# Smoothed int8 layers of a decoder: magnitudes and input integers on ScalarE, roots and weight steps spread from a repeated column

## What is computed

```python
def _smooth_quant_linear(x, w):
    amax_x = max(|x|, axis=0); amax_w = max(|w|, axis=0)
    s = maximum(sqrt(maximum(amax_x, EPS) / maximum(amax_w, EPS)), EPS)
    xs = x / s;  ws = w * s
    x_scale = maximum(max(|xs|, axis=-1), EPS) / 127      # one per row
    w_scale = maximum(max(|ws|, axis=-1), EPS) / 127
    x_q = clip(round(xs / x_scale)); w_q = clip(round(ws / w_scale))
    return x_q @ w_q.T * x_scale * w_scale.T

h = _smooth_quant_linear(x, guw); gate, up = split(h, 2, axis=-1)
a = silu(gate) * up
y = _smooth_quant_linear(a, dw)
```

## Time and profile before

| | |
|---|---|
| median of 3 runs | 1121.04 us (1120.28 to 1121.95) |
| the profiled execution | 1115.83 us, its span 1114.0 us |
| DVE busy | 862.6 us, 77% of the span |
| ACT busy | 555.0 us, 50% |
| PE busy | 798.0 us, 72% |
| the stage that the change touches | about 608.8 to 851.8 us of the span |

### The profile page before, as it was taken

One profiled execution on the slowest core, in us unless ns is written; L12 is line 12 of the kernel. 1 busy time (PEld: TensorE's weight loads), 2 busy tenths in 40 slices (PEclk: granted clock), 3 DMA queues, 4 the chain that ended last, 5 costly groups with the idle time before them and its releaser, 6 DMA issues.

```text
span 1114.0 us, 15206 instructions
## 1 busy us (share of the span) xinstructions
PE 798.0 (72%) x5063; PEld 322.0 (29%) x5063; DVE 862.6 (77%) x1155; ACT 555.0 (50%) x971; POOL 102.3 (9%) x220
## 2 busy tenths in 40 slices
PE   1456987999999999999356244533454266999997
PEld 1422321222222222223111022212224143444443
DVE  6999999999999999985999888898888574322111
ACT  4846324888888888885080024223233652754000
POOL 2110010000000000100000010000101052000001
PEclk9778995999999999999658556666567677999999
DMA  8400770111111121110300011010007402000000
GB/s 300 154 0 1 231 265 30 45 55 52 49 56 44 53 57 45 54 38 16 116 0 1 0 38 38 19 29 1 0 1 290 163 2 76 1 1 1 19 29 29
DMA packets 48323, 66.73 MB, mean 60 GB/s; under 512 B 11532, under 2 KB 25868, under 8 KB 47768
## 3 DMA queue, kind: packets, MB, share of 16 engines
q1 hardware_dynamic: 46488, 61.95, 16.9%
q0 software_dynamic: 1792, 4.22, 1.1%
HBM read 42.52 MB, written 19.19 MB: 55 GB/s over the span
## 4 chain that ended last, share of the span: by engine, by line
PE 46%; DVE 36%; issue 8%; ACT 6%; POOL 2%; DMA 1%; ACTq 1%; POOLq 0%; SPq 0%; DVEq 0%
PE PS L1302 11%; PE PS L1483 8%; PE PS L1493 7%; PE PS L1319 7%; PE PS L1271 5%; PE PS L1238 2%; ACT slab L1590 2%; DVE slab L999 2%; DVE slab L956 2%; DVE SWV L855 2%; DVE stats L663 2%; DVE HB L927 2%; ACT HB L1581 2%; DVE slab L989 2%; DVE mn L690 1%
## 5 line engine op out<-in xcount | busy, mean ns | idle before, releaser
L855 DVE TENSOR_REDUCE SWV<-PS 128x2 f32<-128x1024 f32 x256 | 303.3, 1219 | 22.2 <-PE PS L1271 18.8
L1590 ACT ACTIVATE slab<-PS 128x512 f32<-128x512 f32 x512 | 273.4, 600 | 77.7 <-PE PS L1319 71.6
L1302 PE MATMUL PS<-slab,HB 128*32 128x256 f32 x2048 | 157.6, 392 | 5.9 <-ACT HB L1581 5.9
L1319 PE MATMUL PS<-slab 50*128 50x512 f16 x512 | 139.4, 387 | 12.8 <-ACT slab L1590 10.5
L1271 PE MATMUL PS<-slab 48*128 48x512 f16 x512 | 103.9, 403 | 11.3 <-DVE SWV L855 10.2
L1483 PE MATMUL PS<-slab 128*128 128x512 f16 x384 | 86.5, 389 | 1.4 <-DVE slab L1138 1.4
L1493 PE MATMUL PS<-slab 128*128 128x512 f16 x384 | 83.0, 379 | 0.0
L1611 ACT ACTIVATE slab<-slab,rnd,inv 128x512 f32<-128x512 f32 (+1 forms) x32 | 20.0, 696 | 108.9 <-DVE inv L985 108.9
L1302 PEld LDWEIGHTS PS<-slab,HB 128*32 128x32 f32 x2048 | 45.0, 108 | 77.0 <-issue 70.0
L1153 DVE SCALAR_TENSOR_TENSOR slab<-HB,cmax,slab 128x512 f16<-128x512 f32 x32 | 24.1, 752 | 53.7 <-ACT slab L1658 53.7
L1319 PEld LDWEIGHTS PS<-slab 50*128 50x128 f16 x512 | 39.0, 94 | 72.7 <-ACT slab L1590 66.7
(11 more groups left out here) (273 smaller groups left out, 1227.4 us busy)
## 6 DMA issues: line engine op xcount, KB each, us to landing
slab<-in_L_ffn_w SPq DMA_DIRECT2D x2, 4096.0 KB, 13.6
q_split<-slab SPq DMA_DIRECT2D x24, 256.0 KB, 2.7
k_split<-slab SPq DMA_DIRECT2D x24, 256.0 KB, 2.8
slab<-q_split SPq DMA_DIRECT2D x64, 96.0 KB, 2.5
slab<-k_split SPq DMA_DIRECT2D x64, 96.0 KB, 2.5
slab<-in_x SPq DMA_DIRECT2D x4, 1024.0 KB, 12.3
slab<-HB SPq DMA_DIRECT2D x128, 32.0 KB
slab<-in_fside_BxS2xS SPq DMA_DIRECT2D x4, 1024.0 KB, 5.3
```

The costliest lines, as they stand in the source:

```text
L855: nc.vector.tensor_reduce(NM[:, ring].rearrange("p (a x) -> p a x", a=2)[:, :, x], PS[:, bank:bank + 2, :], AX.X, ALU.max, negate=True).th ...
L1302: ins = nc.tensor.matmul(PS[32 * h:32 * h + 32, 6, cols], VST[:, r % 2, k, h, :], PROB[:, k, h, cols], start=k == half == 0, stop=k == KB ...
L1319: nc.tensor.matmul(PS[:, st_bank(2 * s + a), :], KP[rows, r, p, P * k:P * k + P], QP[rows, r, p, :], start=True, stop=True).then_inc(st_re ...
L1590: nc.scalar.activation(PROB[:, k, 2 * a + p], PS[:, st_bank(t), :], ACT.Exp, scale=score_scale).then_inc(probs, 1)
```

## The change

Four things are changed in the stage.

- Column maxima (weights of every step, inputs of wide steps): ScalarE writes magnitudes into two buffers, `ABSW` and `ABSX`, in place of WB's contents (free by then); VectorE takes the larger of tiles 0, 1 and 2, 3 and then of the two results (two `tensor_tensor` instead of one reduction). Inputs of narrow steps keep the reduction.
- ScalarE's magnitudes of the weights of step n + 1 stand at the top of its work for step n, that is behind all of its work for step n - 1.
- No diagonals are built. TensorE takes a column repeated 128 times as weights and the identity as moving operand, one 128-column matmul for each block: eight for the roots of a wide step, four for a narrow one, and four for the row of weight steps. VectorE's L968 and GpSimd's L598 are gone.
- The input's integers are made by ScalarE, ahead of the weights' integers, in the same five-instruction form.
- The loads of router, b1 and b2 wait for the last weights' maxima, and GpSimd's constants for the routing wait likewise, since they write to WB.

```diff
             def weight_maxima(n):
-                dve.wait_ge(lw_in[n % 4], 16 * (n // 4 + 1))
-                nc.vector.tensor_reduce(LWM[chain(n)][:, 0:width(n)],
-                                        LW[chain(n)][layer(n)].rearrange("p t d -> p d t"), AX.X, ALU.max,
-                                        apply_absolute_value=True).then_inc(l_wmax, 1)
+                dve.wait_ge(l_wabs, n + 1)
+                largest_of_tiles(LWM[chain(n)][:, 0:width(n)], absolute(ABSW, n), l_wmax)
...
+            def largest_of_tiles(dst, a, signal):
+                own(nc.vector.tensor_tensor(a[:, 0:2], a[:, 0:2], a[:, 2:4], ALU.max))
+                nc.vector.tensor_tensor(dst, a[:, 0], a[:, 1], ALU.max).then_inc(signal, 1)
...
-                own(nc.vector.reciprocal(roots[:, 0, 0:ic], roots[:, 1, 0:ic]))
-                nc.vector.tensor_tensor(DIAG[c][:, 0:2, 0:w].rearrange("p a (i q) -> p a i q", q=P),
-                                        identf[:, :].unsqueeze(1).unsqueeze(1).broadcast_to([P, 2, ic, P]),
-                                        roots[:, :, 0:ic].unsqueeze(3).broadcast_to([P, 2, ic, P]),
-                                        ALU.mult).then_inc(l_diag, 1)
+                nc.vector.reciprocal(roots[:, 0, 0:ic], roots[:, 1, 0:ic]).then_inc(l_roots, 1)
...
-                for t in range(4):
-                    ins = nc.vector.tensor_scalar(xi[:, t], xi[:, t], lin[c][:, 0, t:t + 1], ROUND, ALU.mult, ALU.add)
-                own(ins)
-                nc.vector.tensor_scalar(LXQ[c][layer(n)], xi, ROUND, None, ALU.subtract).then_inc(l_xq, 1)
...
+            def in_every_row(bank, column):
+                return nc.tensor.matmul(bank, column.broadcast_to([P, P]), identf[:, :], start=True, stop=True)
+
             def spread_roots(n):
...
                 for a in range(2):
-                    nc.tensor.matmul(PS[:, 4 * c + 2 + a, 0:w], ones[:, :], DIAG[c][:, a, 0:w], start=True,
-                                     stop=True).then_inc(l_row, 1)
+                    for i in range(width(n) // P):
+                        ins = in_every_row(PS[:, 4 * c + 2 + a, P * i:P * i + P], roots[:, a, i:i + 1])
+                    ins.then_inc(l_row, 1)
...
+            def magnitude_of_w(n):
+                act.wait_ge(lw_in[n % 4], 16 * (n // 4 + 1))
+                if n:
+                    act.wait_ge(l_wmax, n)
+                nc.scalar.activation(absolute(ABSW, n), LW[chain(n)][layer(n)], ACT.Abs).then_inc(l_wabs, 1)
...
             for n in range(LSTEPS):
-                c, a = chain(n), layer(n)
+                if n + 1 < LSTEPS:
+                    magnitude_of_w(n + 1)
+                    if layer(n + 1) == 0:
+                        magnitude_of_x(n + 1)
+                c, a, xi = chain(n), layer(n), xin(n)
                 act.wait_ge(l_scale, n + 1)
+                for t in range(4):
+                    nc.scalar.activation(xi[:, t], xi[:, t], ACT.Identity, bias=rnd[:, 0:1],
+                                         scale=lin[c][:, 0, t:t + 1]).then_inc(l_xscaled, 1)
+                act.wait_ge(l_xscaled, 4 * n + 4)
+                nc.scalar.activation(LXQ[c][a], xi, ACT.Identity, bias=rnd[:, 1:2]).then_inc(l_xq, 1)
```

More of the change, by code:

```diff
@@ L140, in decoder_kernel, with absolute @@
         LWT = [[turned(m, 3072, w) for w in DIN] for m in OWN_SLAB]
-        LXM = [slab[m][:, 2048:2560] for m in OWN_SLAB]
+        LXM = [slab[m][:, 6144:6656] for m in OWN_SLAB]
         LH = [tiles(m, 4096, D) for m in OWN_SLAB]
-        DIAG = [slab[m][:, 6144:7680].rearrange("p (a d) -> p a d", a=3) for m in OWN_SLAB]
         ROWW = [slab[m][:, 7680:8192] for m in OWN_SLAB]
+        ABSW, ABSX = (wide.rearrange("p (t d) -> p t d", t=4) for wide in (wbf[:, 0:2048], wbf[:, 2048:4096]))
+        def absolute(where, n):
+            return where[:, :, 0:width(n)]
         def xin(n):
@@ L1413, in _ @@
                 c, ic, more = chain(n), width(n) // P, n + 1 < LSTEPS
-                pe.wait_ge(l_diagw, n + 1)
-                nc.tensor.matmul(PS[:, 4 * c, :], ones[:, :], DIAG[c][:, 2], start=True, stop=True).then_inc(l_rowt, 1)
+                pe.wait_ge(l_scale, n + 1)
+                for t in range(4):
+                    ins = in_every_row(PS[:, 4 * c, P * t:P * t + P], lsc[c][:, 1, t:t + 1])
+                ins.then_inc(l_rowt, 1)
                 if more:
@@ L1605, in silu, with magnitude_of_x @@
                 nc.scalar.activation(gate, gate, ACT.Silu).then_inc(l_silu, 1)
-            for n in range(LSTEPS):
-                c, a = chain(n), layer(n)
-                act.wait_ge(l_scale, n + 1)
+            def magnitude_of_w(n):
[3 more added lines that the diff above has]
+                nc.scalar.activation(absolute(ABSW, n), LW[chain(n)][layer(n)], ACT.Abs).then_inc(l_wabs, 1)
+            def magnitude_of_x(n):
+                before = 2 * (n // 4) + chain(n)
+                act.wait_ge(l_h2, 4 * before + 4)
+                if n:
+                    act.wait_ge(l_max, 4 * (n // 4) + chain(n) if chain(n) else n - 2)
+                nc.scalar.activation(absolute(ABSX, n), xin(n), ACT.Abs).then_inc(l_xabs, 1)
+            magnitude_of_w(0)
+            magnitude_of_x(0)
+            for n in range(LSTEPS):
+                if n + 1 < LSTEPS:
[3 more added lines that the diff above has]
+                c, a, xi = chain(n), layer(n), xin(n)
+                act.wait_ge(l_scale, n + 1)
+                for t in range(4):
+                    nc.scalar.activation(xi[:, t], xi[:, t], ACT.Identity, bias=rnd[:, 0:1],
+                                         scale=lin[c][:, 0, t:t + 1]).then_inc(l_xscaled, 1)
+                act.wait_ge(l_xscaled, 4 * n + 4)
+                nc.scalar.activation(LXQ[c][a], xi, ACT.Identity, bias=rnd[:, 1:2]).then_inc(l_xq, 1)
                 for t in range(4):
```

38 lines of the change are left out of this document (18 added, 20 removed).

## The result

The changed kernel takes **1134.84 us** (median of 4 runs, 1133.08 to 1136.76) against 1120.66 (4 runs, 1119.14 to 1121.95): a ratio of 1.0132 with a 95% interval of 1.0110 to 1.0154, or **14.2 us slower**. The direction is as forecast and the time lies within the range; the forecast of 1142.0 was 7 us too high.

What follows compares the result with a forecast made beforehand. VectorE was taken to bound the stage: 45.0 (magnitude waits) + 22.9 (silu) + 1.0 + 2.3 (small waits) - 49.2 (work removed) = +22.0 us, from 1121.0 to 1143.0, less 1 for overlaps: 1142 us, range 1128 to 1160.

Steps and rivals of the forecast that it cites:

- The bound: In the stage, VectorE (busy 217.0 of 246.0 us) sets the time; work leaving it shortens the stage unless it then waits.
- VectorE gives up 49.2 us: VectorE in the stage: maxima, diagonals and input integers leave or shrink, 49.2 us less work.
- Six waits for the magnitudes, 45.0: VectorE, steps 1 to 6: idles through spread, turn, copy and magnitude before the next weights' maxima, 45.0 us more.
- fast TensorE: Rival: TensorE at 2.4 GHz shortens spread and turn in the six waits; +8, some 1129 us; chance 0.12, mixes included.
- The column form costs nothing: TensorE's spread of the roots: 16 small passes take 3.7 us wide against 3.78 before, so no added time.
- Slow passes: Rival: every change of weights on TensorE costs, lengthening the spread; 1148 to 1175 us; chance 0.18.
- the rule that I had set against the form: TensorE's full-height weight loads never overlap matmuls in flight, so a pass would take 0.55 us.
- Silu, 22.9 more: VectorE's gating multiply, steps 1, 2, 5, 6: waits for silu behind both tensors' rounding on ScalarE, 27.4 us instead of 4.5.
- Small terms: VectorE's waits for turned maxima in step 1, 1.0 us more, and at step 7's last product, 2.3 more; loads nothing.
- GpSimd's diagonal leaves a path that was hidden: nothing: Removing GpSimd's diagonal for the row of weight steps was priced at no gain.
- The sum: Whole stage: 45.0 + 22.9 + 1.0 + 2.3 - 49.2 = +22.0 us, 1143.0, less 1 for overlapping ends.
- The other side, 1098: Rival: the magnitude is there when VectorE asks, so the six waits vanish; 23 us gained, 1098 us; chance 0.05.

Runs made afterwards that it cites:

- e1: The kernel before with the column form alone (no diagonals, roots and weight steps spread by repeated-column matmuls): 1099.87 us, ratio 0.9876.
- e3: The kernel before with only the magnitudes moved to ScalarE, the weights' at the top of its step: 1140.36 us, ratio 1.0233.
- e7_after: The changed kernel itself, nothing altered, measured again in a later set of runs: 1136.05 us, ratio 1.0146 to the kernel before.
- e5_silu: The changed kernel with silu set between ScalarE's rounding of the input and of the weights: 1121.95 us, ratio 1.0017 to the kernel before.
- e11_vec_top: The changed kernel with the inputs' integers left on VectorE: 1129.70 us, ratio 1.0082 to the kernel before.
- e2: The kernel before with only the inputs' integers moved to ScalarE, ahead of the weights': 1113.02 us, ratio 0.9994.
- e4_early: The changed kernel with the weights' magnitude made two steps ahead, before ScalarE's row copy: 1096.14 us, ratio 0.9837 to the kernel before.
- e8: The kernel before with only GpSimd's diagonal removed, TensorE making the row of weight steps from a repeated column: 1112.18 us, ratio 0.9926.
- e9: The changed kernel with the inputs' integers left on VectorE and the weights' magnitude made early: 1089.05 us, ratio 0.9717 to the kernel before.

## Why the prediction was right, and where it was not

**The bound.** VectorE bound the stage, and work taken off it counted only where no wait replaced it. Right: e1 and e3 are each explained by VectorE's work and waits alone (e3: -16.6 + 42.6 = 26.0, measured 25.9).

**VectorE gives up 49.2 us.** Busy time fell by 50.4. The maximum over 256 columns, which no row had shown and which I put at 0.42 between 0 and 0.69, is 424 ns:

```profile
L925 DVE TENSOR_TENSOR HB<-WB 128x256 f32<-128x256 f32 x4 | 1.7, 424 | 0.1
```

**Six waits for the magnitudes, 45.0.** They came six times, in the steps named, 40.4 in sum: 7.97, 6.72, 5.88, 7.16, 5.89, 6.73 against 8.6, 6.95, 6.1, 7.8, 8.6, 6.95. Most of it is one round, step 5, 5.89 instead of 8.6. TensorE's timeline, first in step 1, then in step 5:

```profile
650.04 3.78 PE L1387 MATMUL PS<-identf,mx 128*128 128x128 f32 x16 [0.40 <-DVE mx L972]
653.62 1.46 PE L1406 MATMUL PS<-identb,slab 128*128 128x128 bf16 x16
...
775.36 2.05 PE L1387 MATMUL PS<-identf,mx 128*128 128x128 f32 x16 [1.80 <-DVE mx L972]
777.25 1.06 PE L1406 MATMUL PS<-identb,slab 128*128 128x128 bf16 x16
```

The same 16 passes and 16 transposes take 3.78 and 1.46 there, 2.05 and 1.06 here. The busy time by stretch gives the granted clock of the two, and of what went before the second (the columns are those of the first fence; PEclk is third from the end):

```profile
650.00:653.60 3.60, 3.56 (x16) 3.51 (x17) 0.00 (x0) 3.57 (x4) 0.00 (x0) 0.50 0.00 0
```

```profile
766.00:770.00 4.00, 3.19 (x12) 2.50 (x12) 3.94 (x7) 3.71 (x5) 0.00 (x0) 0.50 0.01 2
770.00:773.40 3.40, 2.66 (x21) 2.49 (x20) 2.12 (x4) 3.40 (x5) 0.00 (x0) 0.50 0.00 0
...
775.40:778.30 2.90, 2.90 (x32) 2.72 (x32) 0.00 (x0) 2.90 (x3) 0.00 (x0) 1.00 0.00 0
```

TensorE had been busy 5.85 of the 7.4 us up to 773.4 at 1.2 GHz, and was at 2.4 GHz when the spread came. In e7_after the same two rows are 2.05 and 1.06 again. So **the step that failed** is the size of this term: every round was priced at the low clock ("the rows used are mostly at the low level"), and of the rival "fast TensorE" it was said "For it: none, since TensorE has the same work in a longer stage with longer gaps". A stage mean of 0.63 says nothing about a single round.

Other kernels with the same magnitudes at the top of the step show that the wait follows TensorE's two rows (step 5, us; the last column is the wait less the two):

| kernel | spread | turn | wait | rest |
|---|---|---|---|---|
| after | 2.05 | 1.06 | 5.89 | 2.78 |
| e5_silu | 3.45 | 1.06 | 7.29 | 2.78 |
| e3_magnitudes | 3.17 | 1.59 | 7.50 | 2.74 |
| e11_vec_top | 3.78 | 1.35 | 7.87 | 2.74 |

The last of them, on TensorE's timeline and on VectorE's:

```profile
779.14 3.78 PE L1393 MATMUL PS<-identf,mx 128*128 128x128 f32 x16 [1.80 <-DVE mx L972]
```

```profile
786.96 0.69 DVE L924 TENSOR_TENSOR WB<-WB 128x512 f32<-128x512 f32 x1 [7.87 <-ACT WB L1620]
```

And the trace of the kernel before had a warning, behind the steps whose rows I used. In its step 5 the spread is 3.45 and the turn 1.32, where I took 3.78 and 1.91:

```profile
773.19 3.45 PE L1394 MATMUL PS<-slab,ones 128*128 128x512 f32 x4 [3.06 <-DVE slab L968]
776.43 1.32 PE L1406 MATMUL PS<-identb,slab 128*128 128x128 bf16 x16
```

One round of six at the high level is worth (3.78 - 2.05) + (1.91 - 1.06) = 2.6 us; steps 1 and 4, whose turns took 1.46 (not 1.91) and 0.64 (not 1.06), are 0.4 each. The remaining 1.2 is a fifth of a microsecond a round, and e11_vec_top bears that out: in its step 1 both rows are at the low level (3.78 and 1.91) and the wait is 8.43, not 8.6. My reading, which no run tests, is that I had added the tails of rows that the next row overlaps.

**The column form costs nothing.** Right: the wide spread was forecast at "some 3.8" with 16 rows and took 3.78. "Slow passes" is ruled out, and so is the rule that I had set against the form (the Trainium skill, page "TensorE: Matmul & The Clock Gate", Part 3, "What overlaps and what doesn't"): at 0.55 for a pass the row would have been 8.8 us. In e1_column no wide spread takes more than 3.78 either, and VectorE's wait for the roots' rows is 2.5 us there as before.

**Silu, 22.9 more.** Measured 27.5 - 4.5 = 23.0, with 9.65, 4.81, 8.23 and 4.81 against 9.6, 4.8, 8.2 and 4.8. Read off the queue: ten instructions of known length, less a product of known length.

**Small terms.** Turned maxima +0.8 (1.0 forecast), last product 2.9 (2.3): near enough. For the transfers nothing was forecast, and none of VectorE's waits in the stage is for one. "GpSimd's diagonal leaves a path that was hidden: nothing" was **wrong as a statement**, since it cost VectorE 7.0 us in the kernel before. That no number of the sum moved by it is luck: the change takes away both the diagonal and the four instructions that it held up. I had read GpSimd's work for who waits on it, and nobody does; I had not asked what runs beside it. The 25.6 us that I put down to the integers' move contain these 7: with the diagonal gone only 19 were left for the move. So the single parts, -14.8 + 0.3 + 25.8 = +11.3 of stage, do not add up to the +16.1 of the whole: the move takes 25.4 off VectorE in e2 and only 19.0 once the column form is in, 6.4 that both parts count. The whole is 4.8 above the sum, not 6.4; its waits for magnitudes are 2.9 shorter than e11's (40.4 against 43.3), which is the clock of steps 1, 4 and 5 again. Of the 1.3 that remain, 0.7 are e11's waits against e3's (43.3 and 42.6); the other 0.6 are open.

**The sum.** -50.4 + 40.4 + 23.0 + 0.8 + 2.9 - 0.3 (two waits for the roots' row, 2.5 before and 2.2 now) = 16.4, measured 16.1 of stage and 14.2 and 15.6 by medians. Of the 5.6 between this and the forecast 22.0, 4.6 are the magnitudes' waits and 1.2 the busy time; the other terms were together 0.2 too low. The 1 us that I took off for overlapping ends went the right way and was too little. The first median, 1134.84, lies at the lower edge of the forecast's own band (1134 to 1148): what came is that forecast with a part of "fast TensorE" in it.

**The other side, 1098.** It needed the magnitude to be there when VectorE asks, and I gave it 0.05 because the queues say the reverse. e4_early puts the magnitude in another place of the queue and comes to 0.9837 of before, 18.3 us faster where 23 had been forecast for that case. Between it and the changed kernel lie 34 us, not the 45 of the six waits: they were only 40.4, and 5.3 us of waits are left in e4. The queue's order alone decided the sign.

## What to carry to other kernels

When work moves to an idle engine, what it costs is set by its place in that engine's in-order queue, not by that engine's load: list what stands ahead of it, and ask whether any of that waits, through however many engines, for the one being relieved. Put what the bound engine asks for next (here the magnitude, then silu) ahead of what it needs later, and price the move again after that. And before a small instruction on another engine is called free because nobody waits for it, look whether an instruction that runs beside it is slower than its like elsewhere.

## What the runs showed of the hardware that was not expected

- A GpSimd `tensor_tensor` of 1.04 us beside four VectorE `tensor_scalar` on SBUF stretched those from 1.68 to 2.55 us (128x512 each) and from 1.14 to 2.02 (128x256). The means of one were 697 or 698 and 564 ns in the two kernels that had the diagonal beside them (before, e3), and 482 to 484 and 349 or 350 ns in the four kernels without it (e1, e8, e9, e11).
- f32 matmuls of 128 columns, each with its own full-height weight load, ran as 16 passes in 3.78 us at 1.2 GHz and in 2.05 at 2.4 (0.24 and 0.13 a pass, the row's end included): no slower than the four passes of 512 columns that gave the same result in 3.78 us.
- In the changed kernel TensorE's clock stood at 2.4 GHz for one of the four wide spreads (2.05 us in place of 3.78), at the same place in both of its executions, in a stage whose mean was 0.61. In e11_vec_top the spread at that place took 3.78 us.
